# A displaced 5x5 convolution with group norm: the row matrices' fills spread over three engines, two small distance steps moved from GpSimd to VectorE, and stores issued later in a step

## The chip, the cores and the metric

One core of one Trainium2 chip runs the whole kernel. The metric is device time of one execution, in microseconds (us), as the median of three runs. The kernel before takes 1196.63 us (1196.0 to 1199.26).

## The reference, cut to what matters

Input x has shape (32, 384, 64, 64), float32. Channels belong to 48 positions of 8 channels. `offset` (48 x 2) is rounded: the whole part displaces the position's images (zeros come in at the edge), the fraction shifts the centre of a normalised 5x5 Gaussian.

```python
xn = group_norm(x, G=32, eps=1e-5)        # 12 channels of one image in a group
disp = shift(xn, round(offset))           # zeros outside
d = field5x5 + (offset - round(offset))
kernel = exp(-sum(d * d) / 0.5);  kernel /= kernel.sum()
out = x + depthwise_conv(disp, kernel, padding=2)
```

A Gaussian is a product of a row part and a column part, and both a shift and a 1D convolution are 64 x 64 matrices. So a position is two matrix products, one over rows and one over columns.

## The kernel before, in words

**Tiles.** The 384 channels are cut into 16 superblocks (`c`) of 24 channels, which are 3 positions. The 32 images are cut into 16 steps (`s`) of 2 images. A step's tile `xin[:, s]` has 128 partitions (2 images, 16 blocks of 4 rows, 4 lanes of channels) and 1536 elements each. All 16 steps of a superblock have a slot of their own in `xin`; TOTAL is 256 steps, `t = 16c + s`, and two steps make a pair (`PAIR`).

**TensorE** runs `two_steps` (L675) 128 times. In the order of its own queue, for the even step and then the odd one: `y_product` for positions 0, 1, 2 multiplies the normalised tile `norm` by the row matrices `ay` (128 matmuls a step); between them `sum_stats` (L650, 8 matmuls) sums the statistics of a later pair over partitions; then `x_products` (L669, 96 matmuls a step) multiplies the copied result `y` by the column matrices `ax`, and the next pair's first `y_product` closes the round (`begin_even`, L673). Both steps' y products come before both steps' x products. I call "a pair" the stretch from one start of the x products (L669 x192) to the next.

**ScalarE** has, per step (`step` of its block, L607): `copy_y` (L581: PSUM to `y`, all 4 lanes of an even step, 3 of an odd one), `store` (L605: two output DMAs of the step two back, `BEHIND`), `normalise` (L570: the first half of the channels, two steps ahead) and, in odd steps, `copy_third` (L599) for the even and the odd step: a third of the x products goes to `x2` for GpSimd to add. After steps 5, 7 and 9 it squares `t_int` and `t_full` (L549) and takes the exponential (L553) for the next superblock. At a border (s = 15) `fill_rows` (L559) writes the next superblock's row matrices `ay` from `t_msk`: 3 positions x 2 images, 128 x 256 elements each, written with a stride of two.

**VectorE** has: `copy_last_lane` (L474) of the odd step's y, `add_x` (L481) of both steps, six `statistics` (L453) of a pair eight steps ahead with `sums` (L463: reduces what `sum_stats` made) between the fifth and the sixth, and after s = 11 `values` (L440), which makes `t_msk` for the next superblock.

**GpSimd (POOL)** has, per step, `normalise` (L316: the second half of the channels); in odd steps `coefficients` (seven small operations, L291 to L302), `make_summands` (L274, L276: what `sum_stats` reads) and two `add_third` (L307); after s = 3 and s = 5 `whole_distances` (L247) and `full_distances` (L255) for the next superblock; after s = 15 `column_matrices` (L263).

**What orders the work.** Every engine's program is written out by hand, with semaphores between engines. The waits that matter here: TensorE starts `sum_stats` only after `summands_ready`, the x products only after `ax_ready`, `sums_ready` and `y_ready`, the odd step's x products only after `last_lane_ready`, and the next pair's y products only after `x2_ready` (`copy_third` of the even step), `result1_ready` (`add_x` of the even step) and `mats_ready[0]`:

```python
def two_steps(one):
    ...
    y_product(1, 0)
    pe.wait_ge(summands_ready, one)
    sum_stats(0)
    pe.wait_ge(mats_ready[2], one)
    y_product(2, 0)
    ...
    x_products(1)
    pe.wait_ge(x2_ready, two)
    pe.wait_ge(result1_ready, two)
    begin_even(three)
```

SyncE loads `xin` slot by slot, each after the landing of that slot's store.

Of the kernel before, what the change touches and what calls it, by code (L numbers as in the profile page):

```python
# [6 lines left out]
ALU = mybir.AluOpType  # L7
# [3 lines left out]
BATCH, CH, HW = 32, 384, 64  # L11
P = 128
POSITIONS = 48
B = 2
# [32 lines left out]
def displaced_conv(nc: bass.Bass, x: bass.AP, offset: bass.AP, out: bass.AP):  # L47
# [7 lines left out]
    with ExitStack() as ctx:  # L55
# [3 lines left out]
        def sem(name):  # L59
            return ctx.enter_context(nc.semaphore(name))  # L60
# [83 lines left out]
        norm0_ready = sem("norm0_ready")  # L144
        norm1_ready = sem("norm1_ready")
        norm1_free = sem("norm1_free")
        y_done = sem("y_done")
        y_ready = sem("y_ready")
        last_lane_ready = sem("last_lane_ready")
# [16 lines left out]
        exp_ready = sem("exp_ready")  # L166
        made = sem("made")
        mats_ready = [sem(f"mats{k}_ready") for k in range(POS)]
        ax_ready = sem("ax_ready")

        block = ctx.enter_context(nc.Block())
# [41 lines left out]
        def _(pool):  # L213
# [26 lines left out]
            pool.wait_ge(filled, FILLS)  # L240

            def whole_distances(c):
                if c is 0:
                    pool.wait_ge(shifts, 1)
                else:
                    pool.wait_ge(made, c)
                pool.tensor_tensor(t_int[:], grid[:, None, :, :].to_broadcast([P, POS, KINDS, HW]),  # L247
                                   place[:, bass.ds(POS * c, POS), :].unsqueeze(3).to_broadcast([P, POS, KINDS, HW]),
                                   ALU.add).then_inc(dist_ready, 1)

            def full_distances(c):
                if c is 0:
                    pool.wait_ge(fractions, 2)
                pool.wait_ge(dist_ready, 2 * c + 1)
                pool.tensor_tensor(t_full[:], t_int[:],  # L255
                                   sub5[:, bass.ds(POS * c, POS), :].unsqueeze(3).to_broadcast([P, POS, KINDS, HW]),
                                   ALU.add).then_inc(dist_ready, 1)

            def column_matrices(c):
                pool.wait_ge(made, c + 1)  # L260
                if c is not 0:
                    pool.wait_ge(x_done, ADDS * STEPS * c)
                pool.tensor_tensor(ax[:], t_msk[:, :, R, :],  # L263
                                   gain[:, bass.ds(POS * c, POS)].unsqueeze(2).to_broadcast([P, POS, HW]),
                                   ALU.mult).then_inc(ax_ready, STEPS)
# [58 lines left out]
            coefficients(0, 0, early=True, used=False)  # L324
            for s in range(PAIR):
                normalise(s, s, 0, first=True)
            column_matrices(0)
            make_summands(1, 1, early=True)
            coefficients(1, 1, early=True, used=False)
# [2 lines left out]
            def step(c, s, head, tail):  # L332
                t, p = STEPS * c + s, STEPS // PAIR * c + s // PAIR
                if not (tail and s + PAIR >= STEPS):
                    normalise(t + PAIR, (s + PAIR) % STEPS, STEPS // PAIR * c + (s + PAIR) // PAIR)
                if s % PAIR == 1:
                    if not (tail and s // PAIR + LEAD >= STEPS // PAIR):
                        coefficients(p + LEAD, (s // PAIR + LEAD) % 2)
                    if not (tail and s // PAIR + LEAD + 1 >= STEPS // PAIR):
                        make_summands(p + LEAD + 1, (s // PAIR + LEAD + 1) % RING)  # L340
                    else:

                        pool.engine_nop().then_inc(summands_ready, PAIR)
                    add_third(t - 1, s - 1)
                    add_third(t, s)
                if not tail:
                    if s == 3:
                        whole_distances(c + 1)
                    if s == 5:
                        full_distances(c + 1)  # L350
                    if s == STEPS - 1:
                        column_matrices(c + 1)
            run(step)

        @block.vector
        def _(dve):
# [14 lines left out]
            def shift_and_fraction():  # L371
# [47 lines left out]
                settle()  # L419
                nc.vector.engine_nop().then_inc(shifts, 1)  # L420

            def gain_sums():
                dve.wait_ge(taps_exp, 1)
                own(nc.vector.tensor_reduce(tap_sum[:].rearrange("p n k -> p (n k)"),
                                            tap_e[:].rearrange("p t m -> p m t"), AX.X, ALU.add))
# [8 lines left out]
            def values(c):  # L434

                dve.wait_ge(exp_ready, c + 1)
                if c is not 0:
                    dve.wait_ge(ax_ready, STEPS * c)
                    dve.wait_ge(mats_ready[POS - 1], STEPS * c)
                nc.vector.scalar_tensor_tensor(out=t_msk[:].rearrange("p a k w -> p (a k w)"),  # L440
                                               in0=t_isq[:].rearrange("p a k w -> p (a k w)"), scalar=4.0,
                                               in1=t_exp[:].rearrange("p a k w -> p (a k w)"),
                                               op0=ALU.is_le, op1=ALU.mult).then_inc(made, 1)

            def statistics(c, s, n, pair=None):
                if n == 0:
# [37 lines left out]
            def all_statistics(s):  # L484
                for part in range(CHUNKS):
                    statistics(0, s, part)
# [6 lines left out]
            sums(0, 0, early=True)  # L493
            all_gains()
            values(0)
            all_statistics(2)
            all_statistics(3)

# [13 lines left out]
            def step(c, s, head, tail):  # L512
                t, p = STEPS * c + s, STEPS // PAIR * c + s // PAIR
                if s % PAIR == 0:
                    copy_last_lane(t + 1)
                add_x(t, s)
                if s % PAIR == 1:
                    reduced = None
                    if not (tail and s // PAIR + LEAD + 1 >= STEPS // PAIR):
                        def reduced():  # L520
                            sums(p + LEAD + 1, (s // PAIR + LEAD + 1) % 2, read=True, evicted=t + PAIR)
                    else:
                        nc.vector.engine_nop().then_inc(sums_ready, PAIR)
                    if not (tail and s + AHEAD >= STEPS):
                        pair_statistics(c, s - 1 + AHEAD, p + AHEAD // PAIR, reduced)
                    elif reduced:
                        reduced()
                    if s == 11 and not tail:
                        values(c + 1)
            run(step)  # L530

        @block.scalar
        def _(act):
# [19 lines left out]
                nc.scalar.activation(t_exp[:], t_fsq[:], ACT.Exp, scale=-2.0).then_inc(exp_ready, 1)  # L553

            def fill_rows(c, k):
                if k == 0:
                    act.wait_ge(made, c + 1)
                for part in range(B):
                    filled_k = nc.scalar.activation(ay[:, k].rearrange("p r (m b) -> p (r m) b", b=B)[:, :, part],  # L559
                                                    t_msk[:, k, 0:R].rearrange("p r m -> p (r m)"), ACT.Identity,  # L560
                                                    scale=same[:, part:part + 1])
                filled_k.then_inc(mats_ready[k], STEPS)
# [26 lines left out]
            fill_rows(0, 0)  # L589
            normalise(0, 0, 0, True)  # L590
            fill_rows(0, 1)
            fill_rows(0, 2)
            normalise(1, 1, 0, True)

            def copy_third(t, s, first=False):
# [11 lines left out]
            def step(c, s, head, tail):  # L607
                t = STEPS * c + s
                copy_y(t, s % 2, head and s <= 1)
                if s >= BEHIND:  # L610
                    store(c, s - BEHIND, t - BEHIND)
                elif not head:
                    store(c - 1, s - BEHIND + STEPS, t - BEHIND)
                border = s == STEPS - 1 and not tail
                if border:
                    fill_rows(c + 1, 0)
                if s % PAIR == 1:
                    copy_third(t - 1, s - 1, head and s == 1)
                if border:
                    fill_rows(c + 1, 1)  # L620
                    copy_third(t, s)
                    fill_rows(c + 1, 2)
                if not (tail and s + PAIR >= STEPS):
                    normalise(t + PAIR, (s + PAIR) % STEPS, STEPS // PAIR * c + (s + PAIR) // PAIR, False)
                if s % PAIR == 1 and not border:
                    copy_third(t, s, head and s == 1)
                if not tail:
                    if s == 5:
                        square(c + 1, 0)
                    if s == 7:  # L630
                        square(c + 1, 1)
                    if s == 9:
                        exponential(c + 1)
# [10 lines left out]
        def _(pe):  # L644
# [29 lines left out]

            def begin_even(number):  # L675
                pe.wait_ge(norm0_ready, number)
                pe.wait_ge(mats_ready[0], number)
                y_product(0, 0)

# [75 lines left out]
```

## Time and profile before

| | us |
|---|---|
| median of three runs | 1196.63 (1196.0 to 1199.26) |
| the profiled execution, its own time | 1197.39 |
| its span | 1195.6 |
| TensorE matmul busy | 1174.4 (98%) |
| VectorE busy | 912.0 (76%) |
| ScalarE busy | 793.6 (66%) |
| GpSimd busy | 973.5 (81%) |

The rest of the 1197.39 lies around the span. A busy share says how long an engine had an instruction running. Matmuls overlap and their ends are modelled, so a wait shorter than a few hundred ns shows better in the starts of the groups of matmuls than in idle time. An entry such as "[0.66 <-ACT x]" is the idle time before an instruction and what ended it. ACTq is ScalarE's sequencer: it issues the store DMAs.

### The profile page before, as it was taken

To read this page: it belongs to the slowest core of one execution; us is meant where nothing else is said; L and a number is where in the kernel's file an instruction comes from. 1 tells how busy PE (TensorE), PEld (TensorE's weight loads), DVE (VectorE), ACT (ScalarE), POOL (GpSimd) and SP (SyncE) were. 2 spreads that over 40 slices of the span, in tenths; PEclk is the share of its full clock that TensorE was granted. 3 is DMA by queue.
4 is the path that set the end of the run, shared out by engine and by line. 5 is a ranking of instruction groups with operands and counts; after the bars stand their busy time and mean duration, and the time that the engine had idled before them with its cause. 6 is when DMAs were issued, how large, how long until landed. Compare 5 with 4: busy or idle time off the path is not lost.

```text
span 1195.6 us, 114437 instructions
## 1 busy us (share of the span) xinstructions
PE 1174.4 (98%) x50736; PEld 1144.7 (96%) x50736; DVE 912.0 (76%) x1327; ACT 793.6 (66%) x921; POOL 973.5 (81%) x1741
## 2 busy tenths in 40 slices
PE   9899999999999999999999999999999999999997
PEld 9899999999999999999999999999999999999997
DVE  6687787777778778787777877777777787877773
ACT  3567666666766776667676666676666766667754
POOL 5787888879788888978878887887888888888884
PEclk9999999999999999999999999999999999999999
DMA  8599999999999999999999999999999999999956
GB/s 266 173 383 383 368 358 345 351 352 348 354 341 349 348 341 351 344 352 348 346 347 350 350 349 346 346 346 355 345 349 345 347 347 354 341 354 344 354 199 211
DMA packets 409761, 402.94 MB, mean 337 GB/s; under 512 B 16528, under 2 KB 409744, under 8 KB 409744
## 3 DMA queue, kind: packets, MB, share of 16 engines
q1 hardware_dynamic: 204944, 201.41, 51.6%
q10 hardware_dynamic: 204800, 201.36, 49.1%
q8 instruction: 4, 0.07, 0.0%
q14 instruction: 13, 0.11, 0.0%
HBM read 201.38 MB, written 201.33 MB: 337 GB/s over the span
## 4 chain that ended last, share of the span: by engine, by line
PE 87%; POOL 3%; issue 3%; ACTq 3%; ACT 1%; POOLq 0%
PE ps L658 57%; PE ps L669 27%; ACTq L605 2%; PE ps L650 2%; POOL t_full L255 1%; ACT x L599 1%; ACT ay L559 1%; POOL norm L316 1%; POOL rstd L300 1%; POOL xin L307 0%; POOL summands L274 0%; POOL summands L276 0%; POOL spread L296 0%; POOL var L298 0%; POOL inner L293 0%
## 5 line engine op out<-in xcount | busy, mean ns | idle before, releaser
L658 PE MATMUL ps<-ay,norm 32*128 32x128 f32 x24608 | 755.8, 274 | 8.8 <-ACT x L599 7.9
L658 PEld LDWEIGHTS ps<-ay,norm 32*128 32x128 f32 x24608 | 716.2, 187 | 18.3 <-issue 10.5
L581 ACT ACTIVATE y<-ps 128x1536 f32<-128x1536 f32 (+1 forms) x256 | 330.2, 1290 | 251.3 <-PE ps L658 251.3
L453 DVE BATCH_NORM_STATS2 stats<-xin 128x6 f32<-128x512 f32 x768 | 487.6, 692 | 3.3 <-DMA xin<-in_x_dram 3.3
L669 PE MATMUL ps<-ax,y 64*64 64x64 f32 x24576 | 404.0, 220 | 2.0 <-issue 2.0
L669 PEld LDWEIGHTS ps<-ax,y 64*64 64x64 f32 x24576 | 384.9, 135 | 19.1 <-issue 2.3
L481 DVE TENSOR_TENSOR xin<-ps,xin 128x1024 f32<-128x1024 f32 x256 | 313.5, 1224 | 89.0 <-PE ps L669 88.6
L316 POOL TENSOR_SCALAR norm<-xin,rstd,bias 128x768 f32<-128x768 f32 x256 | 260.7, 1020 | 121.5 <-PE ps L658 103.3
L307 POOL TENSOR_TENSOR xin<-x,xin 128x512 f32<-128x512 f32 x256 | 320.1, 1272 | 7.4 <-ACT x L599 7.2
L570 ACT ACTIVATE norm<-xin,bias,rstd 128x768 f32<-128x768 f32 x256 | 261.7, 1022 | 35.2 <-issue 34.5
L599 ACT ACTIVATE x<-ps 128x512 f32<-128x512 f32 x256 | 151.2, 591 | 83.4 <-PE ps L669 83.3
L463 DVE TENSOR_REDUCE both<-ps 128x12 f32<-128x144 f32 x128 | 39.4, 308 | 140.8 <-ACT y L581 134.9
L300 POOL TENSOR_TENSOR rstd<-var,mhalf 128x4 f32<-128x4 f32 x128 | 130.2, 1017 | 10.0
L474 DVE COPY y<-ps 128x384 f32<-128x384 f32 x128 | 71.3, 557 | 41.2 <-PE ps L658 41.2
L559 ACT ACTIVATE ay<-t_msk,same 128x256 f32<-128x256 f32 x96 | 44.7, 522 | 17.8 <-issue 10.4
L650 PE MATMUL ps<-summands,ones 32*128 32x36 f32 x1040 | 47.4, 246 | 3.2 <-POOL summands L276 2.9
L650 PEld LDWEIGHTS ps<-summands,ones 32*128 32x128 f32 x1040 | 43.4, 188 | 6.1 <-POOL summands L276 5.5
L276 POOL TENSOR_TENSOR summands<-stats 128x12 f32<-128x12 f32 x128 | 27.2, 213 | 19.8 <-POOL summands L274 19.6
L296 POOL TENSOR_TENSOR spread<-inner,both 128x4 f32<-128x4 f32 x128 | 26.0, 203 | 10.7
L298 POOL TENSOR_TENSOR var<-spread,mean_sq 128x4 f32<-128x4 f32 x128 | 26.4, 206 | 10.0
L293 POOL TENSOR_SCALAR inner<-both 128x4 f32<-128x4 f32 x128 | 25.4, 199 | 10.8
L302 POOL TENSOR_TENSOR bias<-minus_mean,rstd 128x4 f32<-128x4 f32 x128 | 25.5, 199 | 10.0
(58 smaller groups left out, 282.7 us busy)
## 6 DMA issues: line engine op xcount, KB each, us to landing
xin<-in_x_dram SPq DMA_DIRECT2D x512, 384.0 KB, 7.3
out_dram<-xin ACTq DMA_DIRECT2D x512, 384.0 KB, 7.4
off<-in_L_conv_offset_dram SPq DMA_DIRECT2D x1, 48.0 KB, 3.2
```

The source lines that it names most:

```text
L300: pool.tensor_tensor(rstd[:, v], var[:, v], mhalf[:, :], ALU.pow).then_inc(small, 1)
L307: pool.tensor_tensor(at, x2[:, s % 2], at, ALU.add).then_inc(result0_ready, 1)
L316: pool.tensor_scalar(norm[:, s % 2, :, cols].rearrange("p r (q w) -> p q r w", w=HW), xin[:, s, QG:].rearrange("p q (r w) -> p q r w", w=H ...
L453: nc.vector.bn_stats(stats[:, s // PAIR % RING, s % PAIR, n, :], xin[:, s].rearrange("p (g q) f -> p q f g", g=GROUPS)[:, n]).then_inc(bn_ ...
L474: nc.vector.tensor_copy(y[:, 1].rearrange("p k r a m -> p a (k r) m")[:, LANES - 1], ps[:, 1, LANES - 1, 0:POS * P].rearrange("p (n m) -> ...
L481: nc.vector.tensor_tensor(at, ps[:, s % 2, 0:2].rearrange("p h (k f) -> p h k f", k=2), at, ALU.add).then_inc(result1_ready, 1)
L570: nc.scalar.activation(norm[:, s % 2, :, cols].rearrange("p r (q w) -> p q r w", w=HW), xin[:, s, 0:QG].rearrange("p q (r w) -> p q r w", ...
L581: nc.scalar.activation(y[:, v].rearrange("p k r a m -> p a (k r) m")[:, 0:lanes], ps[:, v, 0:lanes, 0:POS * P].rearrange("p a (n m) -> p a ...
L599: nc.scalar.activation(x2[:, s % 2], ps[:, s % 2, 2:4, 0:ROW], ACT.Copy).then_inc(x2_ready, 1)
L650: last = nc.tensor.matmul(ps[:, v, a, SUMS], ones[rows, :], summands[rows].rearrange("p t n s -> p (t n s)"), start=True, stop=True)
L658: last = nc.tensor.matmul(ps[:, v, a, P * k:P * (k + 1)], norm[rows, v, r, P * k:P * (k + 1)], ay[rows, k, r, :], start=(r == 0), stop=(r ...
L669: last = nc.tensor.matmul(ps[outs, v, 2 * (k // 2) + h, at:at + HW], y[rows, v, k, r].rearrange("p a m -> p (a m)")[:, outs], ax[rows, k], ...
```

## The change

1. The six fills of `ay` are shared: VectorE does image 0 of position 0 (`fill_image`, in s = 14 behind `copy_last_lane`, with a new semaphore `half0_ready`), GpSimd both images of position 2 (`fill_rows`, in s = 15 between `normalise` and `coefficients`), ScalarE the other three. At the start GpSimd's stand between its first two `normalise`, VectorE's behind `values(0)`.
2. `whole_distances`, `full_distances` and `values` of the next superblock run on VectorE after the fifth `statistics` and ahead of `sums`, in s = 3, 5 and 11. Before, the first two were GpSimd's and the third stood behind the sixth `statistics`.
3. ScalarE's store is issued behind `copy_third` of the even step in odd steps (before: behind `copy_y`); at a border it is issued behind both `copy_third` and `normalise`. In even steps its place stays.

```diff
@@ gpsimd
+            def fill_rows(c):
+                pool.wait_ge(made, c + 1)
+                if c is not 0:
+                    pool.wait_ge(y_done, STEPS * c)
+                pool.sem_inc(rows2_free, 1)
+                for part in range(B):
+                    filled_k = pool.tensor_scalar(ay[:, POS - 1].rearrange("p r (m b) -> p (r m) b", b=B)[:, :, part],
+                                                  t_msk[:, POS - 1, 0:R].rearrange("p r m -> p (r m)"),
+                                                  same[:, part:part + 1], 0.0, ALU.mult, ALU.add)
+                filled_k.then_inc(mats_ready[POS - 1], STEPS)
...
             for s in range(PAIR):
                 normalise(s, s, 0, first=True)
+                if s == 0:
+                    fill_rows(0)
...
                     normalise(t + PAIR, (s + PAIR) % STEPS, STEPS // PAIR * c + (s + PAIR) // PAIR)
+                if s == STEPS - 1 and not tail:
+                    fill_rows(c + 1)
                 if s % PAIR == 1:
...
-                if not tail:
-                    if s == 3:
-                        whole_distances(c + 1)
-                    if s == 5:
-                        full_distances(c + 1)
-                    if s == STEPS - 1:
-                        column_matrices(c + 1)
+                if s == STEPS - 1 and not tail:
+                    column_matrices(c + 1)
@@ vector
+            def whole_distances(c):
+                nc.vector.tensor_tensor(t_int[:], grid..., place..., ALU.add).then_inc(dist_ready, 1)
+            def full_distances(c):
+                dve.wait_ge(dist_ready, 2 * c + 1)
+                nc.vector.tensor_tensor(t_full[:], t_int[:], sub5..., ALU.add).then_inc(dist_ready, 1)
...
-                    dve.wait_ge(mats_ready[POS - 1], STEPS * c)
+                    for k in range(POS):
+                        dve.wait_ge(mats_ready[k], STEPS * c)
...
+            def fill_image(c):
+                dve.wait_ge(made, c + 1)
+                nc.vector.tensor_scalar(ay[:, 0].rearrange("p r (m b) -> p (r m) b", b=B)[:, :, 0],
+                                        t_msk[:, 0, 0:R].rearrange("p r m -> p (r m)"),
+                                        same[:, 0:1], 0.0, ALU.mult, ALU.add).then_inc(half0_ready, STEPS)
...
             values(0)
+            fill_image(0)
...
                 if s % PAIR == 0:
                     copy_last_lane(t + 1)
+                    if s + PAIR == STEPS and not tail:
+                        fill_image(c + 1)
                 add_x(t, s)
...
                         def reduced():
+                            if not tail:
+                                if s == 3:
+                                    whole_distances(c + 1)
+                                if s == 5:
+                                    full_distances(c + 1)
+                                if s == 11:
+                                    values(c + 1)
                             sums(p + LEAD + 1, (s // PAIR + LEAD + 1) % 2, read=True, evicted=t + PAIR)
...
-                    if s == 11 and not tail:
-                        values(c + 1)
@@ scalar
             def fill_rows(c, k):
-                if k == 0:
-                    act.wait_ge(made, c + 1)
-                for part in range(B):
+                act.wait_ge(made, c + 1)
+                for part in range(1 - k, B):
...
             fill_rows(0, 1)
-            fill_rows(0, 2)
...
                 copy_y(t, s % 2, head and s <= 1)
-                if s >= BEHIND:
-                    store(c, s - BEHIND, t - BEHIND)
-                elif not head:
-                    store(c - 1, s - BEHIND + STEPS, t - BEHIND)
                 border = s == STEPS - 1 and not tail
                 if border:
                     fill_rows(c + 1, 0)
                 if s % PAIR == 1:
                     copy_third(t - 1, s - 1, head and s == 1)
                 if border:
                     fill_rows(c + 1, 1)
                     copy_third(t, s)
-                    fill_rows(c + 1, 2)
-                if not (tail and s + PAIR >= STEPS):
+                    normalise(t + PAIR, (s + PAIR) % STEPS, STEPS // PAIR * c + (s + PAIR) // PAIR, False)
+                if s >= BEHIND:
+                    store(c, s - BEHIND, t - BEHIND)
+                elif not head:
+                    store(c - 1, s - BEHIND + STEPS, t - BEHIND)
+                if not border and not (tail and s + PAIR >= STEPS):
                     normalise(t + PAIR, (s + PAIR) % STEPS, STEPS // PAIR * c + (s + PAIR) // PAIR, False)
                 if s % PAIR == 1 and not border:
                     copy_third(t, s, head and s == 1)
@@ tensor
             def begin_even(number):
                 pe.wait_ge(norm0_ready, number)
+                pe.wait_ge(half0_ready, number)
                 pe.wait_ge(mats_ready[0], number)
```

## Rows read from the trace of the kernel before

**Rows 1.** The waits, whole span: engine line waited for: us in total, times, longest us
```profile
PE ps L658 <- ACT x L599: 7.9, 16, 0.8
...
PEld ps L650 <- POOL summands L276: 5.5, 12, 2.1
```
**Rows 2.** The timeline, TensorE, an undisturbed pair: start us, us, engine line op tiles
```profile
74.29 3.03 PE L669 MATMUL ps<-ax,y 64*64 64x64 f32 x192
77.25 2.08 PE L658 MATMUL ps<-ay,norm 32*128 32x128 f32 x64
...
83.05 3.04 PE L669 MATMUL ps<-ax,y 64*64 64x64 f32 x192
```
**Rows 3.** The timeline, a border pair (s = 14 and 15 of one superblock)
```profile
172.95 3.03 PE L669 MATMUL ps<-ax,y 64*64 64x64 f32 x192
...
173.27 1.61 ACTq L605 DMA_DIRECT2D out_dram<-xin  x2
...
174.99 0.94 ACT L559 ACTIVATE ay<-t_msk,same 128x256 f32<-128x256 f32 x2 [0.78 <-issue]
...
175.83 0.57 ACT L599 ACTIVATE x<-ps 128x512 f32<-128x512 f32 x1
...
176.64 2.09 PE L658 MATMUL ps<-ay,norm 32*128 32x128 f32 x64 [0.66 <-ACT x L599]
...
177.20 0.21 POOL L276 TENSOR_TENSOR summands<-stats 128x12 f32<-128x12 f32 x1 [0.15 <-POOL summands L274]
...
178.52 0.35 PE L650 MATMUL ps<-summands,ones 32*128 32x36 f32 x8
...
182.46 3.11 PE L669 MATMUL ps<-ax,y 64*64 64x64 f32 x192
```
**Rows 4.** The timeline, the pair behind `full_distances` (s = 6 and 7)
```profile
209.33 3.03 PE L669 MATMUL ps<-ax,y 64*64 64x64 f32 x192
...
214.64 0.43 PE L650 MATMUL ps<-summands,ones 32*128 32x36 f32 x8 [0.27 <-POOL summands L276]
...
218.64 3.11 PE L669 MATMUL ps<-ax,y 64*64 64x64 f32 x192
```
**Rows 5.** The timeline around `values` (s = 11 to 13)
```profile
158.86 3.13 DVE L453 BATCH_NORM_STATS2 stats<-xin 128x6 f32<-128x512 f32 x5
...
161.98 1.01 POOL L316 TENSOR_SCALAR norm<-xin,rstd,bias 128x768 f32<-128x768 f32 x1
162.89 0.31 DVE L463 TENSOR_REDUCE both<-ps 128x12 f32<-128x144 f32 x1 [0.91 <-ACT y L581]
...
163.73 1.14 DVE L440 SCALAR_TENSOR_TENSOR t_msk<-t_isq,t_exp 128x960 f32<-128x960 f32 x1
163.89 3.22 PE L669 MATMUL ps<-ax,y 64*64 64x64 f32 x192
...
164.20 1.53 POOL L316 TENSOR_SCALAR norm<-xin,rstd,bias 128x768 f32<-128x768 f32 x1 [1.21 <-PE ps L658]
...
164.79 0.55 DVE L474 COPY y<-ps 128x384 f32<-128x384 f32 x1
```
**Rows 6.** Groups of instructions by shape, GpSimd: xcount | busy us, mean ns | idle
```profile
L316 POOL TENSOR_SCALAR norm<-xin,rstd,bias 128x768 f32<-128x768 f32 x256 | 260.7, 1020 | 121.5 <-PE ps L658 103.3 <-ACT norm L570 15.9 <-issue 1.7
...
L274 POOL TENSOR_SCALAR summands<-stats 128x24 f32<-128x24 f32 x128 | 27.5, 215 | 5.2 <-DVE stats L453 0.4 <-issue 0.3
```
**Rows 7.** The timeline of the start-up, VectorE and GpSimd side by side
```profile
5.54 0.45 POOL L233 CAST grid<-grid_i 128x320 f32<-128x320 int32 x1
5.72 0.53 DVE L409 TENSOR_TENSOR place<-shift,src 128x240 f32<-128x240 f32 x1
...
6.71 0.41 DVE L414 SCALAR_TENSOR_TENSOR valid<-place,ok_hi 128x240 f32<-128x240 f32 x1
6.91 1.25 POOL L238 TENSOR_SCALAR grid<-grid,back 128x256 f32<-128x256 f32 x1
7.16 0.57 DVE L417 SCALAR_TENSOR_TENSOR place<-valid,shift 128x240 f32<-128x240 f32 x1
```

More of the change, by code:

```diff
@@ L146, in displaced_conv @@
         norm1_free = sem("norm1_free")
+        rows2_free = sem("rows2_free")
         y_done = sem("y_done")
@@ L168, in displaced_conv @@
         mats_ready = [sem(f"mats{k}_ready") for k in range(POS)]
+        half0_ready = sem("half0_ready")
         ax_ready = sem("ax_ready")
@@ L242, in whole_distances @@
             def whole_distances(c):
[L243 to L246, printed above, removed]
+                pool.wait_ge(shifts, 1)
                 pool.tensor_tensor(t_int[:], grid[:, None, :, :].to_broadcast([P, POS, KINDS, HW]),
@@ L251, in full_distances @@
             def full_distances(c):
-                if c is 0:
-                    pool.wait_ge(fractions, 2)
+                pool.wait_ge(fractions, 2)
                 pool.wait_ge(dist_ready, 2 * c + 1)
@@ L420, in shift_and_fraction @@
                 nc.vector.engine_nop().then_inc(shifts, 1)
+            def whole_distances(c):
+                nc.vector.tensor_tensor(t_int[:], grid[:, None, :, :].to_broadcast([P, POS, KINDS, HW]),
+                                        place[:, bass.ds(POS * c, POS), :].unsqueeze(3).to_broadcast([P, POS, KINDS, HW]),
+                                        ALU.add).then_inc(dist_ready, 1)
+            def full_distances(c):
+                dve.wait_ge(dist_ready, 2 * c + 1)
+                nc.vector.tensor_tensor(t_full[:], t_int[:],
+                                        sub5[:, bass.ds(POS * c, POS), :].unsqueeze(3).to_broadcast([P, POS, KINDS, HW]),
+                                        ALU.add).then_inc(dist_ready, 1)
             def gain_sums():
@@ L527, in step @@
                         reduced()
-                    if s == 11 and not tail:
-                        values(c + 1)
             run(step)
+            nc.vector.engine_nop().then_inc(half0_ready, 1)
         @block.scalar
```

## The prediction, on record before the changed kernel ran

> **What bounds the kernel now.** The table of the page comes first: TensorE's matmuls are busy 98% of the span, the next engine (GpSimd) 81%. So the time is the length of TensorE's queue plus the places where that queue waits, and nothing that another engine saves counts unless it shortens such a wait. All work of TensorE stays, so I ask next what an undisturbed pair takes, and find it in the timeline: from one start of the x products to the next 83.05 - 74.29 = 8.76 us, of which 2.96 to the next y products [rows 2]. There are 128 pairs, so 1121 us are out of reach. What can be had is in the pairs that are longer. The border pair is 182.46 - 172.95 = 9.51 in the timeline [rows 3], the pair behind the second distance operation 218.64 - 209.33 = 9.31 [rows 4], the pair behind `values` 172.95 - 163.89 = 9.06 [rows 3, 5]. The table of waits says who ends them: ScalarE's third copy (L599), 7.9 us in 16 waits, and GpSimd's summands (L276), 5.5 us in 12, the longest of which, 2.1, lies in the start-up [rows 1]. The 7.9 are nearly all of the 15 borders, 0.53 each.
>
> The rest of the surplus is small gaps inside pairs that no edit addresses. I leave them as they are.
>
> **The change, part by part.**
>
> *Border, ScalarE.* The chain in the timeline [rows 3]: the copy of y ends at 174.21 (174.99 less 0.78 idle), the fill waits for the issue of two stores (from 173.27, 1.61 long) until 174.99, two fills take 0.94, the third copy runs 175.83 to 176.40, and the y products start at 176.64 where 172.95 + 2.96 = 175.91 was due: 0.73 late. New: one fill (0.47) from 174.21, the copy behind it ends at 174.21 + 0.47 + 0.57 = 175.25, 0.66 ahead of need. Fills of position 1 (0.94) end at 176.2, and are wanted half of 1.88 behind 175.91, at 176.85. This wait goes: 7.9 us.
>
> *Border, GpSimd.* Two fills are put between `normalise` and `coefficients`, and behind these stand `make_summands`, for which TensorE's `sum_stats` waits, then both `add_third` and `column_matrices`. The trace has no such fill. From the same operation at 24 elements, 215 ns, and 768 elements, 1020 ns [rows 6], I interpolate 215 + 232 x 1.08 = 466 ns. Bounds: below, a third of the 768-element one, 340 ns; above, the start-up's `tensor_scalar` of 256 elements, 1.25 us [rows 7]. I take 0.47, since that 1.25 overlaps VectorE instructions that could have held it up. Two: 0.93. Today the summands end at 177.20 + 0.21 = 177.41, which is 4.46 behind the start of the x products, and `sum_stats` is due at 2.96 + 1.88 = 4.84 (1.88 from 176.64 to 178.52) [rows 3]. So GpSimd has 0.38 to spare and gets 0.93: they end at 5.39, TensorE waits 0.6 and loses about 0.1 more, because what stands behind a late `sum_stats` starts late too. Per border 0.72 in place of 0.53: over 15, 10.8 for 7.9. **The border is no gain but a loss of 2.9 us**; the wait only changes its name from ScalarE to GpSimd. The later GpSimd work of the border (adds of 2.5, columns 0.5) ends before the next x products need it, as these are late as well.
>
> *Border, VectorE.* `fill_image` stands ahead of `add_x` of step 14. 256 elements at about one per cycle and a start cost, as 240 take 0.41 in [rows 7]: 0.41. It begins when the last lane is copied, in the gap in which VectorE waits for the x products anyway, so I cost it at nothing; if the gap were gone, `result1_ready` would be late by up to 0.4 for the next y products, 6 us over 15.
>
> *Distances off GpSimd.* Each is 1.8 us of GpSimd behind the two adds, so `normalise`, `coefficients` and the summands of the next pair are late. In [rows 4] `sum_stats` idles 0.27 and its pair is 9.31 - 8.76 = 0.55 longer: the pair pays about twice the idle time. The row of waits less its start-up entry gives 5.5 - 2.1 = 3.4 idle [rows 1]; at between one and two times that, I take 5.5 us gained (bounds 3.4 and 6.8).
>
> *`values` earlier.* Today it runs at 163.73 for 1.14, and the last lane's copy waits for it and ends at 165.34, 1.45 behind the x products' start, where the odd half is due at 2.96 / 2 = 1.48 less the semaphore's way; GpSimd's `normalise`, started at 164.20, takes 1.53 and not 1.0, ending 0.86 behind `t_msk` [rows 5]. Surplus of this pair 0.30, of which some 0.07 are the small gaps: 0.23 x 15 = 3.4 us gained.
>
> *The three on VectorE ahead of `sums`.* Cost 1.14 each, as `t_msk` of the same size. VectorE's fifth `statistics` ends at 161.99 and `sums` starts at 162.89, held by the copy of y; it ends at 163.20, 0.69 ahead of the x products at 163.89 [rows 5]. With 1.14 put in, `sums` ends at 161.99 + 1.14 + 0.31 less some overlap, 163.4: still 0.4 ahead. Behind it stand the sixth `statistics` and the last lane's copy, which end at 164.7, 0.8 behind the start, where 1.4 is late. So nothing, as long as VectorE is not held up. Below nothing is excluded, as it only adds work; above, see the first rival.
>
> *Stores later.* In odd steps the issue (about 1.4) moves from ahead of the even third copy to ahead of `normalise` and the odd third copy. `normalise` of that step is wanted two steps on, the odd copy by the y products some 6 us behind the x start; today it ends about 3.9 behind, new about 5. In steps 5, 7, 9 a square or the exponential of 1.0 follows and ends at 6, where the next copy of y is due at 6.3. Cover is thin but holds. On SyncE's queue a slot's load starts 1.7 us later; its reader is steps away. Nothing, and a few late copies less.
>
> *Start-up.* GpSimd's two fills there fit in while TensorE runs its idle products. VectorE's stands ahead of twelve `statistics`, back to back, that the second `sums` waits for: 0.4 lost.
>
> Sum: -5.5 - 3.4 + 2.9 + 0.4 = **-5.6 us**, against 1197.39 of the profiled execution, which is 0.76 above the median. A difference carries over: 1196.63 - 5.6 = 1191.0.
>
> **The rivals.**
>
> *A, VectorE held up by GpSimd.* At the place where the three now stand GpSimd works without a break. Its `normalise` starts at 161.98, and the two-input VectorE operation would start at 161.99 [rows 5]. That the two hold each other up is in the trace: VectorE's L409 takes 0.53 beside a GpSimd cast that ends at 5.99, where the same size (L414) takes 0.41 [rows 7]; `normalise` at 164.20 waits for `t_msk` [rows 5]. If GpSimd's instruction holds until its end at 162.99, the operation ends at 162.99 + 1.0 = 164.0 and `sums` at 164.2, so the x products start 0.3 late. Three times in 15 superblocks: 13 us, 1191.0 + 13 = 1204; as often VectorE will be first, I put it at 1202, slower. It decides from a start of VectorE 0.1 us behind GpSimd's on. Against it: L238 has two scalars to read and lasts 1.25 in all, yet L417 began and ended inside it, with 0.43 left for GpSimd behind it [rows 7], so this kind of GpSimd operation lets VectorE in at one point at least. Chance 0.25.
>
> The Trainium skill, SBUF — State Buffer, section Who interferes with whom, states that a VectorE instruction with two SBUF inputs and a GpSimd one that reads SBUF exclude each other, that the one issued first holds the ports for its whole instruction and the other blocks fully. By that rule the case is A; the trace agrees for L409 and `t_msk`, not plainly for L417.
>
> *B, the fill costs more on GpSimd.* At 0.78 each the border pays 0.6 more, 9 us: 1200. At 1.25 it pays 1.56 more, 23 us: 1214. For it: the only 256-element `tensor_scalar` of GpSimd. Against: the overlap named above, and the line through two other sizes. Chance 0.1.
>
> *C, the gain isn't there.* The pairs get shorter where named, but the small gaps grow (stores and loads meet TensorE's reads at other moments), or ScalarE's thin cover fails: 1196.6. The undisturbed 8.76 of [rows 2] against the usual 8.8 to 9.1 says that such gaps exist; nothing says that they answer to this change. Chance 0.12.
>
> **How the numbers follow.** A measurement of this kernel can tell 0.3%, 3.6 us, from no change: faster is below 1193.0, slower above 1200.2. The forecast has 0.53 and its own range is 1187 to 1194. Faster: nearly all of it and a little of A, 0.52. Same: C, the milder part of A and B, 0.25. Slower: the rest of A and B, 0.23. The range takes in the forecast's own from a little below (the border costs nothing more than today) to A: 1186 to 1203.
>
> **What would show it.** Right: at the border the y products start 2.96 behind the x start, and TensorE's wait on L599 is gone, but a wait of 0.5 to 0.7 on L276 has come, 15 times; GpSimd's fill lasts 0.45 to 0.5; no wait on L276 in the pairs of s = 4 to 7; pair of s = 12, 13 at 8.8 to 8.9; start of the x products never held by `sums`. A: the VectorE operations of 960 elements last 1.5 to 2.1 and x products start late in the pairs of s = 4, 6 and 12. B: L276 waits of over 1 us. The forecast fails if GpSimd's fill is off by 0.2 us or more, or if VectorE is held up.

## The result, and the profile after

The changed kernel takes **1180.74 us** (median of 5 runs, 1179.39 to 1181.68) against 1197.78 (1196.0 to 1200.99): ratio 0.9854, 95% interval 0.9839 to 0.9869, a gain of 17 us where 5.6 were forecast, and below the range. The sign was right, the size three times too small.

The busy line of the page (per engine: busy us, share of the span, instructions) says little, as TensorE is at 98% in both:

```profile
PE 1158.7 (98%) x50736; PEld 1131.0 (96%) x50736; DVE 952.8 (81%) x1373; ACT 787.4 (67%) x873; POOL 972.2 (83%) x1743
```

The waits of TensorE say more. ScalarE's third copy, 7.9 us in 16 waits [rows 1], is gone from the list; GpSimd's summands, at L286 now, have the 15 borders and the start-up:

```profile
PEld ps L689 <- POOL summands L286: 11.4, 16, 1.5
...
PE ps L689 <- POOL summands L286: 8.4, 16, 1.3
```

A border pair in the timeline, with the columns of [rows 3]:

```profile
172.21 3.03 PE L708 MATMUL ps<-ax,y 64*64 64x64 f32 x192
172.52 0.99 POOL L326 TENSOR_SCALAR norm<-xin,rstd,bias 128x768 f32<-128x768 f32 x1 [1.15 <-PE ps L697]
...
172.88 0.77 DVE L470 TENSOR_SCALAR ay<-t_msk,same 128x256 f32<-128x256 f32 x1
...
173.37 0.55 ACT L599 ACTIVATE ay<-t_msk,same 128x256 f32<-128x256 f32 x1
...
173.49 1.02 POOL L264 TENSOR_SCALAR ay<-t_msk,same 128x256 f32<-128x256 f32 x2
...
173.91 0.61 ACT L638 ACTIVATE x<-ps 128x512 f32<-128x512 f32 x1
...
175.17 2.08 PE L697 MATMUL ps<-ay,norm 32*128 32x128 f32 x64
...
177.47 0.21 POOL L286 TENSOR_TENSOR summands<-stats 128x12 f32<-128x12 f32 x1 [0.15 <-POOL summands L284]
...
177.73 0.43 PE L689 MATMUL ps<-summands,ones 32*128 32x36 f32 x8 [0.48 <-POOL summands L286]
...
181.74 0.97 PE L708 MATMUL ps<-ax,y 64*64 64x64 f32 x50
```

Read it as the prediction read [rows 3]. The y products start 175.17 - 172.21 = 2.96 behind the x products: no wait on ScalarE. The summands end 5.47 behind them (forecast 5.39), `sum_stats` starts at 5.52 where 4.84 was due, and the pair is 9.53 long, before 9.51. The wait changed its name and kept its size.

To see all pairs I took each pair's length from the starts of its matmuls and subtracted the undisturbed 8.76; the surplus of 125 pairs (the third to the last but one) is split by where in TensorE's order it lies. (The y products are 96 matmuls a step, not 128: 64 of a pair's stand ahead of `sum_stats` and 128 behind it.) "Small gaps" is the way from the first to the last of the 192 x products, less 2.81 and less a wait for the odd half; "third copy" the way from there to the first y product, less 0.15; "summands" the way from there to `sum_stats`, less 1.89; the rest are the odd half's wait and the late restarts. In us:

| kernel | surplus | small gaps | third copy | summands | odd half |
|---|---|---|---|---|---|
| before | 33.3 | 13.5 | 9.8 | 3.6 | 2.6 |
| changed | 14.6 | 0.8 | 0.0 | 10.6 | 0.9 |
| e1 stores only | 21.6 | 2.3 | 0.0 | 10.7 | 3.7 |
| e2 stores back | 27.5 | 11.8 | 6.9 | 4.1 | 0.7 |
| e3 odd store last | 18.9 | 2.2 | 0.0 | 9.8 | 4.3 |
| e4 fill 2 on ScalarE | 3.9 | 0.8 | 0.0 | 0.6 | 1.4 |
| e5 odd loads later | 69.9 | 5.5 | 48.0 | -2.5 | 16.1 |
| e6 odd store first | 142.3 | 6.0 | 0.0 | 0.8 | 134.3 |
| e7 distances only | 23.5 | 9.6 | 12.4 | -1.1 | 0.5 |
| e8 fills only | 39.3 | 19.9 | 3.6 | 8.5 | 2.7 |
| e9 odd loads nudged | 30.5 | 2.5 | 12.2 | 8.0 | 2.9 |
| e10 no fill sharing | 4.3 | 1.1 | 0.0 | 0.6 | 1.7 |

In e5 and e6 the 5.5 and 6.0 are 0.05 in each pair whose odd half starts late, and no gaps. Each row is one traced execution, so a row can be a few us off the median of its kernel (e8's was 1.5 above it, e7's 1.7 below).

The surprise is one column: 13.5 us of **small gaps**, which the prediction had set aside as answering to no edit, fell to 0.8. Everything forecast is in the others. So the questions are which part removes the gaps, what they are, and what each part is worth alone.

### The profile page after: what moved, and what is told of

It is laid out like the page before. It is cut to its first block, busy times and chain, and to the rows that moved or that the text cites. A ratio compares the mean times of both kernels' runs of the same rounds, so it can differ in the third digit from the quotient of the medians.

```text
span 1177.6 us, 114501 instructions
## 1 busy us (share of the span) xinstructions
PE 1158.7 (98%) x50736; PEld 1131.0 (96%) x50736; DVE 952.8 (81%) x1373; ACT 787.4 (67%) x873; POOL 972.2 (83%) x1743
## 4 chain that ended last, share of the span: by engine, by line
PE 89%; POOL 5%; issue 2%; POOLq 0%; DVE 0%; DVEq 0%
PE ps L697 59%; PE ps L708 29%; PE ps L689 2%; POOL ay L264 1%; POOL rstd L310 1%; POOL summands L284 0%; POOL summands L286 0%; POOL spread L306 0%; POOL inner L303 0%; POOL var L308 0%; POOL minus_mean L302 0%; POOL mean_sq L301 0%; POOL bias L312 0%; DVE xin L510 0%; POOL norm L326 0%
## 5 line engine op out<-in xcount | busy, mean ns | idle before, releaser
L708 PE MATMUL ps<-ax,y 64*64 64x64 f32 x24576 | 389.5, 219 | 2.8 <-issue 2.6
L708 PEld LDWEIGHTS ps<-ax,y 64*64 64x64 f32 x24576 | 371.7, 135 | 18.5 <-issue 3.2
L326 POOL TENSOR_SCALAR norm<-xin,rstd,bias 128x768 f32<-128x768 f32 x256 | 293.2, 1145 | 104.5 <-PE ps L697 87.0
L286 POOL TENSOR_TENSOR summands<-stats 128x12 f32<-128x12 f32 x128 | 27.4, 214 | 19.5 <-POOL summands L284 19.3
L306 POOL TENSOR_TENSOR spread<-inner,both 128x4 f32<-128x4 f32 x128 | 26.2, 205 | 10.7
L303 POOL TENSOR_SCALAR inner<-both 128x4 f32<-128x4 f32 x128 | 25.7, 201 | 10.7
L301 POOL TENSOR_TENSOR mean_sq<-both 128x4 f32<-128x4 f32 x128 | 25.6, 200 | 9.0 <-DVE both L492 9.0
```

The costliest lines, as they stand in the source:

```text
L326: pool.tensor_scalar(norm[:, s % 2, :, cols].rearrange("p r (q w) -> p q r w", w=HW), xin[:, s, QG:].rearrange("p q (r w) -> p q r w", w=H ...
L708: last = nc.tensor.matmul(ps[outs, v, 2 * (k // 2) + h, at:at + HW], y[rows, v, k, r].rearrange("p a m -> p (a m)")[:, outs], ax[rows, k], ...
```

## The experiments

**e1: the third part alone (stores later).**

```diff
                 copy_y(t, s % 2, head and s <= 1)
-                store(...)
                 border = s == STEPS - 1 and not tail
...
                     copy_third(t, s)
                     fill_rows(c + 1, 2)
+                    normalise(t + PAIR, ...)
+                store(...)
```

> The kernel before with the third part alone: stores issued behind the even step's third copy in odd steps. The changed kernel lost its small gaps inside the x products of the odd step (x products to y products 2.96 in nearly every pair, where before 3.0 to 3.2 was usual). Theory S (those gaps come from the store issued just ahead of the x products, and moving it removes them): about 13 us of them go here too, so some 1183 to 1186 against 1197, with the border wait on ScalarE's third copy and the waits on GpSimd's summands behind the distances still there. Theory D (they went because VectorE's and GpSimd's work was rearranged): the gaps stay and the time is 1195 to 1197.

Measured 1185.65 (1184.86 to 1188.03), ratio to before 0.9897 (0.9875 to 0.9919). Theory S holds in its size, with one surprise. The border, with all six fills still on ScalarE, in its timeline:

```profile
530.34 3.03 PE L670 MATMUL ps<-ax,y 64*64 64x64 f32 x192
...
531.52 0.94 ACT L559 ACTIVATE ay<-t_msk,same 128x256 f32<-128x256 f32 x2
532.35 0.57 ACT L599 ACTIVATE x<-ps 128x512 f32<-128x512 f32 x1
...
533.30 2.08 PE L659 MATMUL ps<-ay,norm 32*128 32x128 f32 x64
...
539.10 1.10 PE L670 MATMUL ps<-ax,y 64*64 64x64 f32 x60
```

539.10 - 530.34 = 8.76: this border has no surplus. Taking the store's issue from ahead of the fills is enough to end TensorE's wait for ScalarE there, with no fill moved. My expectation had said that this wait would stay; it went. What stayed, and grew, is the wait for summands behind the distances, now 10.7 us for 3.6. My reading is that GpSimd's lateness is its own, and where gaps no longer delay TensorE, TensorE waits for it instead; e9 shows the same with the stores unmoved.

**e2: the changed kernel with the stores back in their old place.**

```diff
+                store(...)
                 border = s == STEPS - 1 and not tail
...
-                    normalise(t + PAIR, ...)
-                store(...)
-                if not border and not (tail and s + PAIR >= STEPS):
+                if not (tail and s + PAIR >= STEPS):
```

> The changed kernel with the stores back behind the copy of y. Theory S: the small gaps in the odd step's x products return, 13 us or more: 1193 to 1197. Theory D: the gaps stay away, 1181 to 1184. Also, with the gaps VectorE reaches its distance operations later than GpSimd its normalise: if whoever starts first keeps the other out, those operations last about 1.9 instead of 1.15 in some superblocks, sums is late and x products start late in the pairs of s = 4, 6, 12; otherwise they last 1.15.

Measured 1194.43 (1189.69 to 1196.61), ratio 0.9967 (0.9952 to 0.9981). The gaps return (11.8). So the first two parts together are worth 4 us, and the stores' place some 13. Rival A's mechanism shows here. The timeline around `values`:

```profile
524.01 1.00 POOL L326 TENSOR_SCALAR norm<-xin,rstd,bias 128x768 f32<-128x768 f32 x1
524.13 1.89 DVE L462 SCALAR_TENSOR_TENSOR t_msk<-t_isq,t_exp 128x960 f32<-128x960 f32 x1
...
525.94 0.30 DVE L492 TENSOR_REDUCE both<-ps 128x12 f32<-128x144 f32 x1
...
526.34 1.35 PE L707 MATMUL ps<-ax,y 64*64 64x64 f32 x77
```

GpSimd's `normalise` came 0.12 first, VectorE's operation lasted 1.89 and not 1.14, `sums` ended at 526.24 and the x products started 0.1 behind it. 11 of the 46 operations lasted over 1.5 in e2, 7 in e7, 5 in e3, 44 in e6, none in the changed kernel, e4 or e10. In all 67 GpSimd's `normalise` had started first; where VectorE started first its operation took 1.14 to 1.15 on average. In the changed kernel it is the other way round:

```profile
481.57 1.15 DVE L433 TENSOR_TENSOR t_int<-grid,place 128x960 f32<-128x960 f32 x1
481.67 1.92 POOL L326 TENSOR_SCALAR norm<-xin,rstd,bias 128x768 f32<-128x768 f32 x1
...
482.63 0.30 DVE L492 TENSOR_REDUCE both<-ps 128x12 f32<-128x144 f32 x1
...
483.53 3.03 PE L708 MATMUL ps<-ax,y 64*64 64x64 f32 x192
```

VectorE is 0.10 ahead, I take it because neither a gap nor a late odd half delays it, and GpSimd's `normalise` pays 0.9 which it has to spare. The Trainium skill (SBUF — State Buffer, Who interferes with whom) states that a VectorE instruction with two SBUF inputs and a GpSimd one that reads SBUF contend, and that the one issued first has the shared ports for its whole instruction. Both traces agree to about 0.1 us: waiting for the other one's end and then running in full would end VectorE's at 525.01 + 1.14 = 526.15 (measured 526.02) and GpSimd's at 482.72 + 1.0 = 483.72 (measured 483.59).

**e3: does it matter how far apart the stores are?** The changed kernel with the odd store last in its step:

```diff
+                if s % PAIR == 0:
                     store(...)
...
                 if s % PAIR == 1 and not border:
                     copy_third(t, s, head and s == 1)
+                if s % PAIR == 1:
+                    store(...)
```

> The changed kernel with the odd step's store behind both third copies and normalise (border too), about 3.5 behind the x products' start, so that it is only some 2.8 ahead of the even step's store. Theory T (the gaps depend on when a store's data starts to move against the odd step's x products): as the changed kernel, 1179 to 1182, no gaps in the x products. Theory B (they depend on how close together two stores are issued, 2.7 us apart before and 4.4 in the changed kernel): the gaps return somewhere in the pair, 1188 to 1196.

Measured 1186.19 (1184.65 to 1187.65), ratio 0.9897 (0.9877 to 0.9918), between the two. Small gaps are 2.2 us, so nearness of two stores does not make them. The loss of 5 against the changed kernel is mostly in another place: the odd half waits 4.3 instead of 0.9, because the even store's issue is at times slow. One such pair in the timeline:

```profile
117.86 1.98 ACTq L644 DMA_DIRECT2D out_dram<-xin  x2
...
120.00 1.03 ACT L610 ACTIVATE norm<-xin,bias,rstd 128x768 f32<-128x768 f32 x1 [0.88 <-issue]
120.22 1.63 PE L714 MATMUL ps<-ax,y 64*64 64x64 f32 x96
120.94 1.11 ACT L621 ACTIVATE y<-ps 128x1152 f32<-128x1152 f32 x1
...
122.15 0.56 PE L714 MATMUL ps<-ax,y 64*64 64x64 f32 x22 [0.29 <-issue]
```

The two DMAs take 1.98 to issue where 1.4 is usual, `normalise` and the odd copy of y behind it come late, and the odd half of the x products with them. It leaves open what the gaps are.

**e4: GpSimd without fills.** The changed kernel with position 2 back on ScalarE:

```diff
-                if s == STEPS - 1 and not tail:
-                    fill_rows(c + 1)          # GpSimd
...
                     copy_third(t, s)
+                    fill_rows(c + 1, 2)       # ScalarE
```

> The changed kernel with the fills of position 2 back on ScalarE, behind its odd third copy, so that GpSimd has no fills. Theory: at the border sum_stats waits 0.6 to 0.7 for GpSimd's summands because of the two fills of 0.53 ahead of the coefficients; without them this wait goes and ScalarE still has its even third copy ready in time: 15 x 0.75 = 11 us less, 1169 to 1171. Rival: another wait takes its place at the border (position 2's matrices or the odd step's normalise from ScalarE come late): 1176 to 1181.

Measured **1169.96** (1168.77 to 1172.62), ratio to before 0.9769 (0.9748 to 0.9790): 11 us below the changed kernel, as expected. The surplus of 125 pairs is 3.9. No new wait took its place.

**e5: are the gaps the loads' doing?** SyncE's load of a slot goes out when its store has landed, so moving the store moved a load as well. Kernel before, with odd slots' loads held back by a semaphore from ScalarE:

```diff
                     sync.wait_ge(stored[s], 16 * B * c)
+                    if s % PAIR == 1:
+                        sync.wait_ge(gate[s], 16 * B * c)
...
                 copy_y(t, s % 2, head and s <= 1)
+                if s % PAIR == 0 and not (head and s < 5):
+                    act.sem_inc(gate[(s - 5) % STEPS], 16 * B)
```

> The kernel before, stores where they were, with the load of each odd slot held back until ScalarE has copied an even y about 6 us behind an x products' start (a semaphore of its own). In the kernel before those loads go out 0.5 to 1.5 behind the x products' start, because the odd store ahead of them landed then; moving the store moved them too. Theory M (the small gaps come from the loads going out there): the gaps of 0.1 to 0.3 in the odd step's x products go, 1184 to 1187. Theory S2 (they come from the odd store itself, issued 0.2 behind the x products' start): they stay, 1195 to 1199.

Measured 1234.32 (1233.78 to 1234.8), ratio 1.0299 (1.0282 to 1.0316): a miss by both expectations. The second half of the x products takes 1.41 at most, without a gap in all pairs, as theory M had it, but the stores now take longer to issue. From its timeline:

```profile
260.23 3.27 PE L674 MATMUL ps<-ax,y 64*64 64x64 f32 x192
...
260.59 0.92 SPq L199 DMA_DIRECT2D xin<-in_x_dram  x1
...
260.75 2.04 ACTq L608 DMA_DIRECT2D out_dram<-xin  x2
...
262.96 0.60 ACT L602 ACTIVATE x<-ps 128x512 f32<-128x512 f32 x1 [1.18 <-PE ps L674]
...
263.79 2.07 PE L663 MATMUL ps<-ay,norm 32*128 32x128 f32 x64 [0.29 <-ACT x L602]
```

The issue lasts 2.04, the even third copy behind it starts 2.73 behind the x products and TensorE waits for it in most pairs, 48 us over the span; the odd half's wait adds 16. It shows what a store's issue ahead of this copy is worth when it gets slow. It shows one thing more, which theory M does not: the loads did not leave the store's side. In these rows the second load issue of a slot (from 260.59) runs beside the store's (from 260.75); in 81 of 124 pairs a load's issue and the store's first one start within 0.1 us of each other, and no gap follows. One load's issue beside one store's is not enough to make a gap.

**e6: the odd store ahead of the copy of y.**

```diff
+                if s % PAIR == 1:
+                    store(...)
                 copy_y(t, s % 2, head and s <= 1)
```

> The changed kernel with the odd step's store ahead of its copy of y, so issued about 1 us ahead of the x products' start. Theory S2 (a store disturbs the x products from about 1.3 us behind the start of its issue on): now the even step's x products, which were never slowed, take more than 1.41. Theory P (only an issue 0.2 to 1.6 behind the x products' start disturbs): they take 1.41. Under both the odd copy of y comes some 0.4 late and the odd half of the x products waits for it: 1200 or more.

Measured 1306.43 (1302.47 to 1309.44), ratio 1.0893 (1.0865 to 1.0922). Against theory S2: the even half took 1.41 in every pair, though the store was issued just ahead of it. The cost is the odd half's wait, in the timeline:

```profile
304.11 1.39 ACTq L644 DMA_DIRECT2D out_dram<-xin  x2
304.72 1.63 PE L714 MATMUL ps<-ax,y 64*64 64x64 f32 x96
305.66 1.13 ACT L621 ACTIVATE y<-ps 128x1152 f32<-128x1152 f32 x1 [0.73 <-issue]
...
306.89 1.63 PE L714 MATMUL ps<-ax,y 64*64 64x64 f32 x96 [0.55 <-issue]
```

ScalarE copies y only when its sequencer has issued both DMAs, 0.9 behind the x products' start.

**e7 and e8: the other two parts alone.** e7 is the kernel before with `whole_distances`, `full_distances` and `values` moved (the diff's lines for them), e8 with the fills shared.

> The kernel before with the second part alone (distances and values on VectorE ahead of sums). By the prediction: 5.5 + 3.4 = 9 us less, 1188 to 1190. Rival A (VectorE kept out by GpSimd's normalise where that starts first): the operations last up to 1.9 in some superblocks and the gain is 2 to 6 us, 1192 to 1196.

> The kernel before with the first part alone (fills shared by three engines). By the prediction: 2.9 + 0.4 = 3 us more, 1199 to 1202, the border wait on ScalarE's third copy replaced by one on GpSimd's summands. Rival: the border gets shorter, below 1195.

e7: 1190.6 (1188.85 to 1193.62), ratio 0.9943 (0.9926 to 0.9959), 7 us less. e8: 1201.49 (1197.69 to 1203.15), ratio 1.0021 (1.0010 to 1.0031), 2.5 us more. Both lie where they were expected, but the table shows that gaps had a part in each: in e7 they fell by 3.9 us while the wait for the third copy rose by 2.6, in e8 they rose by 6.4 while the two waits together fell by 1.3. In e8's waits both names stand side by side:

```profile
ACT ay L603 <- issue: 11.1, 15, 1.0
...
PEld ps L692 <- POOL summands L290: 9.9, 22, 2.1
...
PE ps L700 <- ACT x L642: 2.3, 8, 0.5
```

ScalarE's fills still wait for the store's issue, 15 times; with one fill fewer ahead of the copy TensorE waits for it less (2.3 for 7.9), but for GpSimd more (9.9 for 5.5).

**e9: the loads moved by 1.8 us, stores unmoved.** Pair by pair the traces had one thing in common: the large gaps stand where a load and the odd store are issued side by side. Kernel before, the three engines' timelines of one pair:

```profile
725.58 3.38 PE L669 MATMUL ps<-ax,y 64*64 64x64 f32 x192
...
725.87 1.39 SPq L198 DMA_DIRECT2D xin<-in_x_dram  x2
...
725.90 1.54 ACTq L605 DMA_DIRECT2D out_dram<-xin  x2
```

The 192 matmuls take 3.38 and not 3.03. The edit is e5's, with the semaphore raised behind `copy_third(t - 1, ...)` for slot `(s - 4) % STEPS`, about 1.9 behind the x products' start.

> The kernel before, stores where they were, with each odd slot's load released by ScalarE behind its even third copy, at some 1.9 behind the x products' start instead of 0.3. In the traces so far the small gaps of 0.2 to 0.35 stand only in pairs where SyncE's two load issues (0.3 to 1.7 behind the start) and ScalarE's two store issues (0.3 to 1.9) run side by side. Theory L (a load and a store issued at the same moment, while x products run, disturb these): the gaps go though the stores stay, 1184 to 1188. Theory S (the place of the store alone): they stay, 1195 to 1199.

Measured 1195.49 (1195.11 to 1196.9), ratio 0.9975 (0.9963 to 0.9986). The same stretch:

```profile
482.76 3.03 PE L674 MATMUL ps<-ax,y 64*64 64x64 f32 x192
...
483.07 1.39 ACTq L608 DMA_DIRECT2D out_dram<-xin  x2
...
484.87 1.81 SPq L199 DMA_DIRECT2D xin<-in_x_dram  x2
```

The store is issued 0.31 behind the x products' start as before, and the gaps are gone: 2.5 us of 13.5. Theory L holds in so far as the gaps need a load and a store in step. The traces of the four kernels with ungated loads and the odd store behind the copy of y (before, e2, e7, e8) say it more sharply. In 119 of their 497 pairs both load issues start within 0.1 us of both store issues; the odd half of the x products loses 0.25 us in these on average, and 89 of the 111 pairs that lose over 0.2 are among them. The other 378 lose 0.07. In e9 no pair is so in step, and none loses over 0.13. The time that theory L gave was wrong: of 11 us of gaps only 3 were gained, since the waits for summands rose from 3.6 to 8.0 and those for the third copy from 9.8 to 12.2: gaps had covered them.

**e10: no fill shared.** Second and third part, all fills on ScalarE.

> Distances and values on VectorE and the stores later, all six fills left on ScalarE as in the kernel before. The border's wait on ScalarE was mostly the stores' issue ahead of the fills (0.78 idle of 0.73 lateness); with the issue gone, two fills ahead of the even third copy end it about 2.8 behind the start, 0.1 late at most. Expected 1170 to 1174, as with the fills of position 2 back on ScalarE, so that sharing the fills costs 9 to 11 us in the changed kernel. Rival: the sharing is needed, the border waits 0.5 on ScalarE: 1177 to 1180.

Measured **1169.65** (1169.31 to 1170.46), ratio 0.9756 (0.9740 to 0.9773), with e4 the best, 11 us below the changed kernel. Its border in the timeline:

```profile
523.85 3.03 PE L678 MATMUL ps<-ax,y 64*64 64x64 f32 x192
...
525.00 0.95 ACT L567 ACTIVATE ay<-t_msk,same 128x256 f32<-128x256 f32 x2
...
525.82 0.58 ACT L607 ACTIVATE x<-ps 128x512 f32<-128x512 f32 x1
...
526.81 2.08 PE L667 MATMUL ps<-ay,norm 32*128 32x128 f32 x64
...
532.61 0.58 PE L678 MATMUL ps<-ax,y 64*64 64x64 f32 x24
```

Two fills ahead of the copy, and the y products still start at 2.96, the pair is 8.76 long. The sharing of the fills was not needed once the store's issue was out of the way, and costs 11 us.

## Why the prediction was wrong

By its own steps, with the forecast, then the measured.

- *Distances off GpSimd, `values` earlier*: -8.9; e7 -7 (interval -9 to -5). The waits named go: summands from 3.6 to -1.1 (forecast 5.5), and the odd half's from 2.6 to 0.5, part of the 3.4. That the sum fits so well has some luck in it, as gaps gave 3.9 and the third copy's wait took 2.6 back.
- *Border, GpSimd*: a wait of 0.6 on the summands, about 0.1 behind it, border dearer by 2.9 - measured 0.68 and 0.1, the border pair 0.11 longer on average (9.52 for 9.41), 1.7 us. The 2.9 set a lateness of 0.72 against 0.53 of idle time, where the same rows have TensorE 0.73 late before the change; late against late the border was forecast to stay as it was. The fill lasts 0.53 for a forecast of 0.47; the 1.25 of [rows 7] was no price for it. Rival B is out.
- *Fills in all*: +3.3; e8 +2.5. The number is near by luck: in the trace the third copy's wait fell by 6.2 and the summands' rose by 4.9; what made e8 slower is that small gaps rose from 13.5 to 19.9, which is what rival C had in mind.
- *First two parts*: -5.6; e2 -4.0 (-5.7 to -2.3).
- *Border, VectorE*: `fill_image` takes 0.77, not 0.41. It starts 0.36 behind GpSimd's `normalise` and ends 0.14 behind that one's end (172.88 + 0.77 against 172.52 + 0.99). The cover held: nothing waits for it.
- *The three on VectorE ahead of `sums`*: 1.14 each, nothing lost. Rival A's mechanism is real (e2, e7, e3, e6). That the order of the two engines fell the good way by 0.1 us in the changed kernel is luck, and e2 shows that it is not safe.
- ***Stores later*: "Nothing, and a few late copies less". This is the step that failed.** Alone it is worth 12 us (e1: gaps 11.2 less, the third copy's wait 9.8 less, the summands' wait 7.1 more), and on top of the others 13 to 14. Two things were missed. First, the 0.78 us in which ScalarE's fill waits for the issue [rows 3] was quoted and then credited to the fills' move; but the fills' move leaves it (e8, 15 times) and shortens TensorE's wait by the one fill alone, while the store's move ends both (e1). Had I taken the store's edit alone through [rows 3], the copy would have ended 174.21 + 0.94 + 0.57 = 175.72, ahead of the 175.91 due, and the border wait would have stood with this step. Second, the sentence "small gaps inside pairs that no edit addresses": I never asked what they were. They summed to 13.5 us, more than the whole gain forecast, and the store's move takes the load and store issues from beside the x products in which the gaps stood.
- Rival C said that the gaps could answer to this change and had them grow. They answered, in the whole change the other way, and in e8 its way. Why sharing the fills alone made them grow no run was built to show; in e8's trace 50 pairs have the issues in step, in that of the kernel before 30.

The two misses do not add up plainly, as e9 and e1 show: gaps hide the waits of engines that keep their own time. Removed alone they give 3 us of 11; removed together with GpSimd's distance work and without its fills, they leave a surplus of 4 us in all (e10).

## What to carry to other kernels

Give every part of a surplus a cause before setting it aside, small regular ones too: sum them and compare with the gain that you forecast. Take each part of a change alone through the critical stretch; where two parts remove the same wait, find which one is needed, because the other may only bring its price (here 11 us for shared fills). On an engine whose sequencer also issues DMAs, an issue ahead of work that another engine waits for is a cost of its own, even if it seems to run beside.

## What the runs showed of the hardware

Where two loads and two stores were issued in step, from 0.3 to 1.9 us behind the start of the x products, the second half of these small matmuls was slower; in the pair shown at e9 all 192 took 3.38 us and not 3.03. The same stores with the loads 1.8 us later did no such thing (e9), nor did one load's issue beside a store's (e5). Two loads at that place with the stores away from it came up in three pairs only (one each in e1, e4 and e10), which lost 0.03 at most: that the loads alone are harmless is hardly tested. In the changed kernel, e1, e4 and e10, 18 pairs have both issues in step from 1.9 us on, and neither the rest of the x products nor the y products behind them lost over 0.05. Through which resource the issues reach TensorE, and why their place in the pair matters, no run here shows. The issue of a store's two DMAs took 1.4 us as a rule. Over 1.9 it took 3 times of 256 in the kernel before, 38 in e6 and 105 in e5; the reason is open. And a two-input VectorE operation and a GpSimd `normalise` are decided by which starts first, be it by 0.1 us, at a price of 0.75 us for the VectorE one or 0.9 for the GpSimd one (e2, changed kernel).
